# A graph attention layer on one core: layer norm in four parts, GpSimd as a helper, q through four banks, and x in groups of four at the end

## The chip, the cores and the metric

The kernel runs on one NeuronCore of a Trainium2 chip. The metric is the device time of one execution in microseconds (us); the median of several executions is compared. Engines are named as in the profile: PE (TensorE matmul), PEld (its weight loads), DVE (VectorE), ACT (ScalarE), POOL (GpSimd) and SP (SyncE, which here only starts transfers).

## What is computed

x has 6250 rows (nodes) of 256 columns. There are 200000 edges, sorted by destination. Cut to what matters:

```python
h = jnp.maximum(_layernorm(x, axis=-1), 0.0)
q = linear(h, wq, bq)
k = linear(h, wk, bk)
v = linear(h, wv, bv)
scores = jnp.sum(q[dst] * k[src], axis=-1) * scale
scores = scores + (edge_weight[:, None] @ we + be)[:, 0]
# softmax of the scores over the edges of each destination, then
out = jax.ops.segment_sum(v[src] * attn[:, None], dst, num_segments=n)
y = layer_norm(h + out + linear(h, ws, bs), g1, b1)
ffn = linear(jax.nn.gelu(linear(y, w_ff1, b_ff1)), w_ff2, b_ff2)
result = x + layer_norm(y + ffn, g2, b2)
```

## The kernel before, in words

The 6250 rows are handled as B = 49 blocks of 128 (the last has 106). The program has three parts in a row; between two of them all engines meet.

**The first part** makes h and q. SP loads x into `acc` in four transfers of 12 blocks (`x_in[0..3]`), then the edge lists: `src` and the edge weights by rows, and `dst` twice (`dst_a` on 125 partitions, `dst_b` on 124 and 1). DVE measures 24 blocks (bn_stats, L485), computes mean and deviation (`layer_variance`, the square root on ACT in `layer_deviation`, `layer_factors`, L240 to L263), and ACT normalises block after block with the ReLU fused (L419), counting `h_done`. A loop of 49 turns (one a block) follows. In a turn PE transposes h of the next block (L625) and multiplies (bias L633, weights L635) to q in PSUM bank 2 or 3; DVE copies the transpose to SBUF (`copy_hT`, L492); ACT and DVE split q into three bf16 parts in a chain of four (ACT L426, DVE L502, ACT L430, DVE L496). The first nine turns also measure three of the other 25 blocks each (L521), and ACT normalises two or three blocks a turn. At fixed turns the edge lists are turned on PE (L640) and copied, and a plan of steps is computed (from turn PLAN + 2, PLAN = 13). SP stores h to DRAM in 13 transfers of four blocks (`store_h`, L294; the last has one), in order, each as soon as its blocks are done.

POOL casts the destinations (L358), compares chunk ends (L363, L364), clears the first 12 blocks of `acc` (`clear(0)`, L380), waits until all of h is in DRAM (`h_out`), starts 32 gathers of h rows for the first eight chunks of edges (L388) and clears the rest of `acc` (L380). Then the part ends.

**The second part** goes over the edges: 391 chunks of 512, in some 440 steps. POOL starts four gathers a chunk (L788); SP tells DVE when a chunk has landed (L752) and POOL when one of eight slots is free (L756).

**The third part** goes over the 49 blocks again. In its first loop PE multiplies the sums with wv (L1393), and DVE adds a row block read back from DRAM (`r_rows`, L1273, four in flight). The second loop is the feed forward (PE L1385, L1411, L1419; ACT L1170; POOL L1231, L1235; DVE L1312, L1318 and bn_stats L1285). In its last 16 turns (MIXED) the final layer norm is applied to two blocks a turn: ACT normalises to `z_unit` (L1165), POOL adds b2 to x read again from DRAM (L1242, into `x_b2`), DVE multiplies by g2 (`scale_z`, L1330) and adds (`add_x`, L1336), SP stores (L1121). x is loaded a block at a time (L1125), and x, `x_b2`, `z_unit` and the output rows each have four slots. When the last block of the second loop has been measured, its deviation and factors follow, and then the last 17 blocks go through the same four operations.

Of the kernel before, what the change touches and what calls it, by code (L numbers as in the profile page):

```python
# [29 lines left out]
def ceil_div(a, b):  # L30
    return -(-a // b)


def gnn_layer(nc, x, src, dst, edge_weight, wq, bq, wk, bk, wv, bv, ws, bs, we, be, g1, b1, g2, b2,
# [22 lines left out]
    XH = 2 * XG  # L57
    MEASURED = ceil_div(B - XH, 3)
    PLAN = 13
# [8 lines left out]
    with ctx:  # L68
# [74 lines left out]
        q_bias = q_rest[:, 1, :]  # L143
# [21 lines left out]
        bias_rest = part(D1)  # L165
        assert used[0] <= ROWS and 3 * HEAD <= 6 * D
# [43 lines left out]
        h_done, hT_ready, hT_copied = sem("h_done"), sem("hT_ready"), sem("hT_copied")  # L210
        h_out = [sem(f"h_out{k}") for k in range(5)]
        q_ready, hi_done, rest_done, mid_done, lo_done = (sem(n) for n in ("q_ready", "hi_done", "rest_done", "mid_done", "lo_done"))
# [15 lines left out]
        def columns(v, n):  # L228
            return v.rearrange("(c p) -> p c", p=P)

# [44 lines left out]
        with nc.Block() as block:  # L275
            @block.sync
            def _(sp):
# [13 lines left out]
                def store_h(k):  # L291
                    first, end = 4 * k, min(4 * k + 4, B)
                    sp.wait_ge(h_done, end)
                    sp.dma_start(h_rows[first * P:end * P, :].rearrange("(b p) d -> p b d", p=P), acc[:, first:end, 0:D]).then_inc(h_out[k // 3], 16)  # L294
# [7 lines left out]
                for k in range(ceil_div(B, 4)):  # L302
                    store_h(k)
# [8 lines left out]
            def _(pool):  # L312
# [44 lines left out]
                pool.wait_ge(list_in, 3 * 16)  # L357
                g.tensor_copy(dst_s[0:EDGE_P, :], dst_a[0:EDGE_P, :]).then_inc(dst_cast, 1)  # L358
# [6 lines left out]
                last.then_inc(ends_compared, 1)  # L365
                pool.wait_ge(tab_copied, 2)
# [15 lines left out]
                clear(0)  # L382
# [6 lines left out]
                for k in range(1, 5):  # L389
                    clear(k)  # L390

            @block.scalar
            def _(act):
# [20 lines left out]

                def normalise(first, end):
                    for b in range(first, end):
                        if b == XH:
                            act.wait_ge(ln_done, 2)
                        nc.scalar.activation(acc[:, b, 0:D], acc[:, b, 0:D], ACT.Relu, bias=nmr[:, b:b + 1], scale=rstd[:, b:b + 1]).then_inc(h_done, 1)  # L419

                def normalised(b):
                    return min(B, 4 + 2 * b if 4 + 2 * b <= XH else XH + 3 * (b - (XH - 4) // 2))

                def first_part(b):
                    act.wait_ge(q_ready, b + 1)
                    nc.scalar.copy(q3[:, b, 0, 0:D1], banks[2 + b % 2][:, 0:D1]).then_inc(hi_done, 1)  # L426
# [9 lines left out]
                act.wait_ge(ln_done, 1)  # L436
                normalise(0, 3)
                first_part(0)
                normalise(3, 4)
                for b in range(1, B):  # L440
                    second_part(b - 1)
# [3 lines left out]
                    normalise(normalised(b - 1), normalised(b))  # L445
                    if b == 4:
                        act.wait_ge(src_in, 3 * 16)
                        nc.scalar.copy(src_f, src_i).then_inc(src_cast, 1)
                    if b == 11:
# [5 lines left out]
                    if b == 13:  # L455
# [3 lines left out]
                    if b == MEASURED:  # L459
                        layer_deviation(act, 1, XH, B)  # L460
# [3 lines left out]
            def _(dve):  # L464
# [17 lines left out]
                for k in range(2):  # L482
                    dve.wait_ge(x_in[k], 16)
                    for b in range(k * XG, (k + 1) * XG):
                        last = nc.vector.bn_stats(stats[:, b, :], acc[:, b, 0:D])  # L485
                last.then_inc(stats_done, 1)
                layer_variance(dve, 0, 0, XH)
                layer_factors(dve, 0, 0, XH)

                def copy_hT(b):  # L490
                    dve.wait_ge(hT_ready, b + 1)
# [6 lines left out]
                def what_is_left(b):  # L498
# [3 lines left out]
                    nc.vector.tensor_tensor(q_rest[:, b % 2, :], banks[2 + b % 2][:, 0:D1], q3[:, b, 0, 0:D1], ALU.subtract).then_inc(rest_done, 1)  # L502
# [8 lines left out]
                for b in range(B):  # L511
                    if b + 1 < B:
                        copy_hT(b + 1)
                    if b >= 1:
                        third_part(b - 1)
                    what_is_left(b)
                    if b < MEASURED:
                        for other in range(XH + 3 * b, min(XH + 3 * b + 3, B)):
                            if other % XG == 0:
                                dve.wait_ge(x_in[other // XG] if other < FULL else x_rest_in, 16)  # L520
                            last = nc.vector.bn_stats(stats[:, other, :], acc[:, other, 0:D])  # L521
                    if b == MEASURED - 1:
                        last.then_inc(stats_done, 1)
                        layer_variance(dve, 1, XH, B)
                    if b == MEASURED:
                        layer_factors(dve, 1, XH, B)
                    if b == 7:
# [3 lines left out]
                    if b == 9:  # L531
# [928 lines left out]
```

## Time and profile before

| | |
|---|---|
| median of 3 runs | 2411.99 us (2410.64 to 2416.51) |
| the profiled execution's own time | 2409.18 us |
| its span, first to last instruction | 2407.3 us |
| busy share | PE 92%, PEld 77%, DVE 73%, POOL 68%, ACT 48% |
| mean granted TensorE clock | 0.983 of full speed |
| first layer norm: variance, square root and factors of 24 blocks | 21.20 to 23.46 us, first normalise at 23.49 |
| end of the q loop (its last DVE operation) | 127.2 us |
| first instruction of the second part | 133.2 us |
| end of DVE's longest wait for r, at block 4 | 2121.2 us |
| normalising one of the last blocks on ACT, start to start | 0.51 us |

The busy shares are means over three parts with different limits. The rows below are read by stretch. Lines (L388) are those of the kernel before; a releaser behind "<-" is the instruction or transfer whose end ended an idle time.

### The profile page before, as it was taken

Reading aid. Unit: us, or ns where it says so; the run is one execution under the profiler, and the core shown is the slowest. Engines: PE = TensorE matmul, PEld = TensorE weight load, DVE = VectorE, ACT = ScalarE, POOL = GpSimd, SP = SyncE. Lnnn points to the kernel's source line nnn. Section 1 sums busy time; section 2 is a strip of 40 time slices with the busy share of each in tenths; the row PEclk is TensorE's granted clock in tenths of the full one; section 3 lists DMA queues with packets and bytes.
Section 4 is the critical chain, followed back from the end, with each engine's and each line's share of the span. In section 5 each row is a group of like instructions: output and inputs, shape, how many; then the busy total and the mean of one; then the engine's idle time right before and its main releaser. Section 6 shows DMA issues by size and latency. Waiting matters only on the chain. (4 is left out here: it accounts for less than half of the span.)

```text
span 2407.3 us, 70152 instructions
## 1 busy us (share of the span) xinstructions
PE 2209.0 (92%) x14709; PEld 1864.0 (77%) x14710; DVE 1753.2 (73%) x7374; ACT 1166.4 (48%) x2875; POOL 1631.0 (68%) x1817
## 2 busy tenths in 40 slices
PE   5779989899999999999999999999999999989994
PEld 4568777777777777877888888888888888877883
DVE  6768667676777777777777877787778887784367
ACT  5545444444444444444444544555545555554454
POOL 3457777777777777777777777777777777402355
PEclk8989999999999999999999999999999999999997
DMA  7434444444444444444444444444444444340024
GB/s 228 135 95 137 137 137 138 139 137 136 137 137 139 136 137 136 139 137 137 139 137 138 138 139 137 138 137 139 137 139 137 139 137 139 93 138 5 0 62 143
DMA packets 148690, 311.05 MB, mean 129 GB/s; under 512 B 34127, under 2 KB 85186, under 8 KB 148665
## 3 DMA queue, kind: packets, MB, share of 16 engines
q0 software_dynamic: 75264, 205.62, 29.1%
q1 hardware_dynamic: 55278, 90.19, 11.4%
q10 hardware_dynamic: 18122, 14.96, 2.0%
q8 instruction: 9, 0.15, 0.0%
q14 instruction: 17, 0.13, 0.0%
HBM read 290.21 MB, written 20.43 MB: 129 GB/s over the span
## 5 line engine op out<-in xcount | busy, mean ns | idle before, releaser
L788 POOL DMA_INDIRECT work<-h_rows,idx x1536 | 1458.5, 950 | 483.0 <-issue 446.4
L876 PE MATMUL bank<-work 128*128 x3520 | 836.4, 380 | 0.0
L967 DVE SCALAR_TENSOR_TENSOR work<-bank,work 128x257 bf16<-128x257 f32 x1764 | 646.8, 425 | 232.9 <-SPq L752 201.6
L813 PE MATMUL bank<-q,onehot 128*128 x5304 | 739.4, 274 | 62.1 <-DVE work L967 50.1
L876 PEld LDWEIGHTS bank<-work 128*128 128x128 f32 x3520 | 634.8, 190 | 78.6
L813 PEld LDWEIGHTS bank<-q,onehot 128*128 128x128 bf16 x5304 | 509.2, 98 | 146.9 <-issue 84.8
L924 ACT COPY work<-bank 128x256 f32<-128x256 f32 x880 | 285.4, 377 | 397.8 <-PE bank L863 393.8
L920 ACT ACTIVATE work<-work 128x1 f32<-128x1 f32 x440 | 129.6, 295 | 622.9 <-DVE work L1033 622.9
L1033 DVE CUSTOM_DVE_ANT_0 work<-bank,work 128x512 f32<-128x512 f32 x440 | 329.8, 750 | 106.1 <-PE bank L819 75.8
L921 ACT ACTIVATE work<-work 128x512 f32<-128x512 f32 x440 | 311.6, 708 | 0.0
L863 PE MATMUL bank<-ident,work 128*128 128x128 f32 x1760 | 266.7, 274 | 29.5 <-ACT work L921 29.5
L819 PE MATMUL bank<-ident,work 128*128 128x128 f32 x1764 | 273.1, 277 | 16.7 <-DVE work L973 7.8
L890 ACT ACTIVATE work<-onehot 128x512 bf16<-128x512 bf16 x442 | 284.6, 644 | 1.6 <-DVE onehot L956 1.6
L863 PEld LDWEIGHTS bank<-ident,work 128*128 128x128 f32 x1760 | 212.7, 140 | 86.0 <-ACT work L921 51.5
L819 PEld LDWEIGHTS bank<-ident,work 128*128 128x128 f32 x1764 | 195.2, 136 | 67.4 <-issue 39.7
L956 DVE TENSOR_SCALAR onehot<-dst_words,node 128x512 bf16 x443 | 167.8, 379 | 74.2 <-issue 48.5
L984 DVE SCALAR_TENSOR_TENSOR acc<-acc,work,bank 128x257 f32 x441 | 211.9, 480 | 8.8 <-issue 3.2
L967 DVE DVE_READ_ACCUMULATOR work<-bank,work 128x1 f32 x1764 | 145.2, 82 | 0.0
L973 DVE TENSOR_TENSOR work<-work,ew_all 128x4 f32<-128x4 f32 x441 | 73.6, 167 | 80.3 <-DVE work L967 38.2
L1170 ACT ACTIVATE work<-bank,bff_col 128x128 f32<-128x128 f32 x196 | 55.9, 369 | 98.6 <-PE bank L1411 98.6
L1411 PE MATMUL bank<-work,dst_words 128*128 128x128 f32 x784 | 97.4, 278 | 2.7 <-DVE work L1312 2.6
L1235 POOL TENSOR_TENSOR work<-work 128x256 f32<-128x256 f32 x49 | 35.7, 729 | 90.2 <-DVE acc L1318 88.2
(190 smaller groups left out, 1570.0 us busy)
## 6 DMA issues: line engine op xcount, KB each, us to landing
dst_words<-dst_short SPq DMA_DIRECT2D x99, 512.0 KB
work<-h_rows,idx POOLq DMA_INDIRECT x1568
bias<-h_rows ACTq DMA_DIRECT2D x56, 128.0 KB
r_rows<-bias ACTq DMA_DIRECT2D x55, 128.0 KB
work<-r_rows SPq DMA_DIRECT2D x49, 128.0 KB, 2.0
acc<-in_x SPq DMA_DIRECT2D x4, 1536.0 KB, 15.4
h_rows<-acc SPq DMA_DIRECT2D x12, 512.0 KB, 4.6
work<-in_x SPq DMA_DIRECT2D x48, 128.0 KB, 2.1
```

The source lines that it names most:

```text
L788: pool.indirect_dma_start(rows[:, u, j, 0:D], None, h_rows, bass.IndirectOffsetOnAxis(idx[:, half, u * J + j:u * J + j + 1], 0)).then_inc( ...
L813: last = nc.tensor.matmul(banks[j][:, 0:D1], onehot[:, k, j, :], q3[:, bass.ds(b, 1), c, 0:D1], start=(c == 0), stop=(c == 2))
L819: last = nc.tensor.transpose(banks[4][:, j * P:(j + 1) * P], score[:, k, j:j + 1].broadcast_to([P, P]), ident[:])
L863: last = nc.tensor.transpose(banks[5 - half][:, j * P:(j + 1) * P], probsT[:, (2 * half + j) * P:(2 * half + j + 1) * P], ident[:])
L876: last = nc.tensor.matmul(banks[6 + k][:, 0:D1], probs[:, j, :], rows[:, bass.ds(slot, 1), j, :], start=(j == 2), stop=(j == 1))
L890: nc.scalar.activation(outside[:, k, :], onehot[:, k].rearrange("p j n -> p (j n)"), ACT.Copy, scale=BIG, bias=-BIG).then_inc(outside_done, 1)
L921: nc.scalar.activation(probsT, masked, ACT.Exp, bias=new_max, scale=-1.0).then_inc(exp_done, 1)
L924: nc.scalar.copy(probs[:, 2 * half:2 * half + 2, :].rearrange("p j n -> p (j n)"), banks[5 - half][:, 0:2 * P]).then_inc(probs_done, 1)
L956: nc.vector.tensor_scalar(onehot[:, k], dst_of[:, bass.ds(at, C)].rearrange("p (j n) -> p j n", j=J), node[:, bass.ds(b, 1)], None, ALU.is ...
L967: last = nc.vector.scalar_tensor_tensor(out=product[:, j, 0:D1], in0=banks[j][:, 0:D1], scalar=SCALE, in1=rows[:, bass.ds(slot, 1), j, :], ...
L984: nc.vector.scalar_tensor_tensor(out=a, in0=a, scalar=decay[:, k:k + 1], in1=banks[6 + k][:, 0:D1], op0=ALU.mult, op1=ALU.add).then_inc(ad ...
L1033: nc.vector.tensor_tensor_reduce(out=masked, in0=banks[4][:], in1=outside[:, k, :], scale=-1.0, scalar=old_max[:, k:k + 1], op0=ALU.add, o ...
```

## The change

In the first part the layer norm is done in four parts (12, 12, 12 and 13 blocks) in place of two. The first needs only the first transfer of x. DVE measures four blocks a turn. POOL normalises blocks 40 to 47, in two groups of four: four times scale and shift, then one maximum with zero over the four; ACT normalises the other 41, three a turn. The cast of `src` goes from ACT to POOL. POOL compares the chunk ends ahead of its waits for the lists, and `clear(0)` goes behind the gathers. q goes through banks 2 to 5, and every step of the split comes a turn or two later in its engine's order. From block 14 on, ACT copies the transposes in place of DVE. The plan starts three turns later (PLAN = 16).

In the third part the r blocks have eight slots in place of four, so do `z_unit` and the output rows (which share the r slots). x comes in groups of four blocks, three groups in flight; b2 is added in place, and a group's slot is loaded again once the last of its four blocks has been added. `layer_variance` of the last 17 blocks goes ahead of the last turn's `scale_z` and `add_x`. The loops of the last stage are written out.

```diff
-    XH = 2 * XG
-    MEASURED = ceil_div(B - XH, 3)
-    PLAN = 13
+    QUARTERS = [(0, XG), (XG, 2 * XG), (2 * XG, 3 * XG), (3 * XG, B)]
+    BY_POOL = range(FULL - 8, FULL)
+    BY_ACT = 14
+    PLAN = 16
+        VARIANCE_AT = [ceil_div(end - XG - 10, 4) for first, end in QUARTERS[1:]]
+        DEVIATION_AT = VARIANCE_AT
@@ SP: the stores of h @@
-                for k in range(ceil_div(B, 4)):
-                    store_h(k)
+                for first in range(0, BY_POOL[0], 4):
+                    store_h(first, first + 4)
+                for first in (BY_POOL[0], BY_POOL[0] + 4):
+                    store_h(first, first + 4)
+                    if first == BY_POOL[0]:
+                        store_h(B - 1, B)
@@ POOL @@
-                pool.wait_ge(list_in, 3 * 16)
-                g.tensor_copy(dst_s[0:EDGE_P, :], dst_a[0:EDGE_P, :]).then_inc(dst_cast, 1)
                 pool.wait_ge(plan_consts, 1)
...
                 last.then_inc(ends_compared, 1)
+                pool.wait_ge(src_in, 3 * 16)
+                g.tensor_copy(src_f, src_i).then_inc(src_cast, 1)
+                pool.wait_ge(list_in, 3 * 16)
+                g.tensor_copy(dst_s[0:EDGE_P, :], dst_a[0:EDGE_P, :]).then_inc(dst_cast, 1)
+
+                pool.wait_ge(ln_done, 4)
+                for n, half in enumerate((BY_POOL[0:4], BY_POOL[4:8])):
+                    for b in half:
+                        last = g.tensor_scalar(acc[:, b, 0:D], acc[:, b, 0:D], rstd[:, b:b + 1], nmr[:, b:b + 1], ALU.mult, ALU.add)
+                    last.then_inc(scaled, 1)
+                    pool.wait_ge(scaled, n + 1)
+                    g.tensor_scalar(acc[:, half[0]:half[-1] + 1, 0:D], acc[:, half[0]:half[-1] + 1, 0:D], 0.0, None, ALU.max).then_inc(h_done_by_pool, 4)
...
-                clear(0)
                 for k in range(4):
                     pool.wait_ge(h_out[k], 3 * 16)
...
-                for k in range(1, 5):
+                for k in range(5):
                     clear(k)
@@ ACT @@
+                def copy_hT(b):
+                    act.wait_ge(q_ready, b - 1)
+                    act.wait_ge(hT_ready, b + 1)
+                    nc.scalar.copy(hT[:, b % 2, :], banks[b % 2][:, 0:D]).then_inc(hT_copied_by_act, 1)
...
-                layer_deviation(act, 0, 0, XH)
+                layer_deviation(act, 0, *QUARTERS[0])
                 normalise(0, 3)
-                first_part(0)
-                normalise(3, 4)
-                for b in range(1, B):
-                    second_part(b - 1)
+                for b in range(B):
+                    if BY_ACT <= b + 1 < B:
+                        copy_hT(b + 1)
+                    if b >= 2:
+                        second_part(b - 2)
...
                     first_part(b)
-                    normalise(normalised(b - 1), normalised(b))
+                    if b in DEVIATION_AT:
+                        turn = DEVIATION_AT.index(b) + 1
+                        layer_deviation(act, turn, *QUARTERS[turn])
+                    normalise(3 * b + 3, 3 * b + 6)
@@ DVE @@
+                measure(0, XG)
+                layer_variance(dve, 0, *QUARTERS[0])
+                measure(XG, XG + 2)
+                layer_factors(dve, 0, *QUARTERS[0])
+                measure(XG + 2, XG + 6)
...
-                    if b + 1 < B:
+                    if b + 1 < BY_ACT:
                         copy_hT(b + 1)
+                    if b >= 3:
+                        third_part(b - 3)
                     if b >= 1:
-                        third_part(b - 1)
-                    what_is_left(b)
+                        what_is_left(b - 1)
+                    measure(XG + 6 + 4 * b, XG + 10 + 4 * b)
@@ PE @@
                 def project(b):
-                    k = b % 2
-                    pe.wait_ge(hT_copied, b + 1)
-                    if b >= 2:
-                        pe.wait_ge(rest_done, b - 1)
+                    q = banks[2 + b % 4][:, 0:D1]
+                    copied(b)
+                    if b >= 4:
+                        pe.wait_ge(rest_done, b - 3)
...
                 for b in range(B):
-                    if b + 1 < B:
-                        transpose_h(b + 1)
+                    if b + 2 < B:
+                        transpose_h(b + 2)
                     project(b)
@@ third part @@
+        RING = 8
+        X_GROUPS = 3
-        r_in = slots(4, D)
+        r_in = slots(RING, D)
-        x_again = slots(4, D)
-        x_b2 = r_in
-        z_unit = slots(4, D)
+        x_again = slots(4 * X_GROUPS, D)
+        z_unit = slots(RING, D)
-        o_rows = slots(4, D)
+        o_rows = r_in
@@ SP @@
+                for b in range(B):
+                    n = rows_of(b)
                     sp.wait_ge(o_done, b + 1)
+                    sp.dma_start(out[b * P:b * P + n, :], o_rows[0:n, b % RING, :]).then_inc(o_stored[b % RING], 16)
+                    if b % 4 == 3 and b // 4 + X_GROUPS <= B // 4:
+                        load_x(b // 4 + X_GROUPS)
@@ POOL @@
-                def add_b2(b, at):
-                    n = rows_of(at)
-                    if not (isinstance(b, int) and b < 4):
-                        pool.wait_ge(o_done, b - 3)
-                    pool.wait_ge(x_back[at % 4], turn4(b, at) * 16 + 32)
+                def add_b2(b):
+                    n, k, g = rows_of(b), b % (4 * X_GROUPS), b // 4
+                    pool.wait_ge(x_back[g % X_GROUPS], 16 + g // X_GROUPS * 16 + 16)
+                    nc.gpsimd.tensor_tensor(x_again[0:n, k, :], x_again[0:n, k, :], row_of["b2"][0:n], ALU.add).then_inc(x_b2_done, 1)
@@ DVE, in the last turns @@
                     if b == B - 1:
                         last.then_inc(stats_done, 1)
+                        layer_variance(dve, 7, EARLY, B)
```

## Rows read from the trace of the kernel before

**Rows 1.** Stretches of the span: busy us (instructions) per engine, granted clock, DMA share, GB/s.
```profile
152.30:2082.00 1929.70, 1836.92 (x12499) 1555.34 (x12497) 1444.60 (x6491) 930.35 (x2272) 1468.68 (x1584) 1.00 0.45 138
...
2381.00:2403.00 22.00, 0.00 (x0) 0.00 (x0) 15.52 (x34) 9.08 (x17) 8.97 (x13) 0.50 0.52 160
```

**Rows 2.** Timeline of POOL in the first part: start, us, instruction, count, wait before.
```profile
48.64 1.52 POOL L358 CAST q<-q 125x1600 int16<-125x1600 int32 x1 [28.43 <-DMA q<-in_dst]
...
81.14 1.18 POOL L388 DMA_INDIRECT work<-h_rows,idx  x1 [21.88 <-DMA h_rows<-acc]
...
121.84 8.37 POOL L380 MEMSET acc<- 128x3084 f32 x4
...
152.35 0.95 POOL L788 DMA_INDIRECT work<-h_rows,idx  x1 [22.15 <-SPq L756]
```

**Rows 3.** Groups on POOL from 48 to 131: busy, mean ns | idle before.
```profile
L388 POOL DMA_INDIRECT work<-h_rows,idx x32 | 31.3, 977 | 31.3 <-DMA h_rows<-acc 21.9 <-issue 8.8 <-PE bank L625 0.6
L380 POOL MEMSET acc<- 128x3084 f32 (+1 forms) x5 | 11.0, 2258 | 0.0
L363 POOL TENSOR_SCALAR onehot<-dst_words,work 128x128 bf16<-128x128 f32 x4 | 2.7, 666 | 0.1
```

**Rows 4.** Waits from 200 to 2050: us in total, times, longest.
```profile
DVE work L967 <- SPq L752: 199.5, 167, 2.5
```

**Rows 5.** Timeline of ACT and SP: the last normalise, and the stores of h.
```profile
75.44 0.60 ACT L419 ACTIVATE acc<-acc,nmr,rstd 128x256 f32<-128x256 f32 x1
...
50.34 26.08 SPq L294 DMA_DIRECT2D h_rows<-acc  x8
```

**Rows 6.** Stretches after the lists have landed, columns as in Rows 1.
```profile
48.60:52.00 3.40, 1.16 (x6) 0.85 (x5) 3.33 (x8) 1.57 (x4) 3.27 (x5) 0.86 0.84 290
52.00:57.00 5.00, 4.25 (x20) 3.42 (x18) 1.62 (x5) 2.32 (x6) 4.91 (x11) 0.75 0.30 104
57.00:60.00 3.00, 1.43 (x11) 1.37 (x12) 1.16 (x3) 3.00 (x8) 2.25 (x1) 1.00 0.00 0
```

**Rows 7.** Timeline of DVE in the first part.
```profile
12.32 4.01 DVE L485 BATCH_NORM_STATS2 stats<-acc 128x6 f32<-128x256 f32 x12 [4.11 <-DMA acc<-in_x]
...
31.46 0.42 DVE L496 TENSOR_TENSOR q<-work,q 128x257 bf16<-128x257 f32 x1
...
32.13 1.07 DVE L521 BATCH_NORM_STATS2 stats<-acc 128x6 f32<-128x256 f32 x3
...
33.44 0.42 DVE L496 TENSOR_TENSOR q<-work,q 128x257 bf16<-128x257 f32 x1
...
48.84 1.35 DVE L261 SCALAR_TENSOR_TENSOR nmr<-mean,rstd 128x25 f32<-128x25 f32 x1
```

**Rows 8.** Timeline of PE in two turns late in the q loop.
```profile
120.55 1.03 PE L635 MATMUL bank<-work 128*128 128x257 f32 x4
...
121.80 1.03 PE L635 MATMUL bank<-work 128*128 128x257 f32 x4
```

**Rows 9.** Waits from 2109 to 2126, the start of the third part.
```profile
DVE work L1273 <- DMA work<-r_rows: 6.4, 4, 3.8
```

**Rows 10.** Timeline of DVE from the last feed forward turn to the end.
```profile
2376.26 0.74 DVE L1330 TENSOR_TENSOR work<-work,bias 128x256 f32<-128x256 f32 x2
...
2377.59 0.18 DVE L240 TENSOR_TENSOR mean<-stats 128x17 f32<-128x17 f32 x1
...
2381.22 0.85 DVE L1330 TENSOR_TENSOR work<-work,bias 128x256 f32<-128x256 f32 x2 [1.15 <-ACT work L1165]
...
2401.99 0.75 DVE L1336 TENSOR_TENSOR work<-work 128x256 f32<-128x256 f32 x2
```

**Rows 11.** Groups from 2381 to 2403: busy, mean ns | idle before, releasers.
```profile
L1330 DVE TENSOR_TENSOR work<-work,bias 128x256 f32<-128x256 f32 (+1 forms) x17 | 10.1, 592 | 7.1 <-DMA out<-work 4.2 <-ACT work L1165 2.8
...
L1242 POOL TENSOR_TENSOR work<-work,bias 128x256 f32<-128x256 f32 (+1 forms) x13 | 9.0, 690 | 12.0 <-DMA work<-in_x 8.8 <-DVE work L1336 3.2
L1336 DVE TENSOR_TENSOR work<-work 128x256 f32<-128x256 f32 (+1 forms) x17 | 7.0, 414 | 0.0
```

More of the change, by code:

```diff
@@ L511, in _ @@
                 for b in range(B):
-                    if b + 1 < B:
+                    if b + 1 < BY_ACT:
                         copy_hT(b + 1)
+                    if b >= 3:
+                        third_part(b - 3)
                     if b >= 1:
-                        third_part(b - 1)
-                    what_is_left(b)
[L517 to L527, printed above, removed]
+                        what_is_left(b - 1)
+                    measure(XG + 6 + 4 * b, XG + 10 + 4 * b)
+                    if b in VARIANCE_AT:
+                        turn = VARIANCE_AT.index(b) + 1
+                        layer_variance(dve, turn, *QUARTERS[turn])
+                    if b - 1 in VARIANCE_AT:
+                        turn = VARIANCE_AT.index(b - 1) + 1
+                        layer_factors(dve, turn, *QUARTERS[turn])
+                    if b == 11:
                         dve.wait_ge(tab_turned, 1)
@@ L1196, in mixed @@
-                def mixed(i, j):
-                    b, at = i * 2 + (B - MIXED + j), B - MIXED + j
-                    if not (isinstance(i, int) and b + 1 >= B):
-                        gelu(b + 1, at + 1)
-                    if not (isinstance(i, int) and b + 3 >= B):
+                layer_deviation(act, 6, 0, EARLY)
+                for j in range(MIXED):
+                    b = B - MIXED + j
+                    if b + 1 < B:
+                        gelu(b + 1, b + 1)
+                    if b + 3 < B:
@@ L1209, in _ @@
[L1209 to L1220 removed]
+                        last_unit(2 * j + c, 2 * j + c)
@@ L1222, in _ @@
+                layer_deviation(act, 7, EARLY, B)
+                act.wait_ge(ln_done, 8)
+                for b in range(EARLY, B):
+                    last_unit(b, b)
             @block.gpsimd
@@ L1348, in mixed @@
-                def mixed(i, j):
-                    b, at = i * 2 + (B - MIXED + j), B - MIXED + j
-                    if not (isinstance(i, int) and b + 2 >= B):
-                        copy_yT(b + 2, at + 2)
-                    last = second_sum(b, at)
-                    if isinstance(i, int) and b == B - 1:
+                layer_factors(dve, 6, 0, EARLY)
+                for j in range(MIXED):
+                    b = B - MIXED + j
+                    if b + 2 < B:
+                        copy_yT(b + 2, b + 2)
+                    last = second_sum(b, b)
+                    if b == B - 1:
@@ L1365, in _ @@
-                if MIXED > 2:
-                    for j in range(2):
-                        mixed(MIXED // 2 - 1, j)
-                layer_variance(dve, 5, EARLY, B)
-                layer_factors(dve, 5, EARLY, B)
-                scale_z(EARLY, EARLY)
-                def third_sum(b, at):
-                    scale_z(b + 1, at + 1)
-                    add_x(b, at)
-                over(dve, EARLY, B - 2, 4, third_sum)
-                third_sum(B - 2, B - 2)
-                add_x(B - 1, B - 1)
+                            step(2 * j + c)
@@ L1380, in _ @@
+                layer_factors(dve, 7, EARLY, B)
+                scale_z(EARLY)
+                for b in range(EARLY, B - 1):
+                    scale_z(b + 1)
+                    add_x(b)
+                add_x(B - 1)
             @block.tensor
```

217 lines of the change are left out of this document (100 added, 117 removed).

## The prediction

> **What bounds the kernel now.** I read the stretches of the span first, then POOL's timeline, then who waits for what at the start and at the end.
>
> From 152.3 to 2082 us the edges are worked through [rows 1]. PE is busy 95% of it, but a busy PE in this profile is not one at its peak; POOL is busy 1468.7 of 1929.7 us with 0.3 us of issue between two gathers, and DVE waits 199.5 us for chunks that have not landed [rows 4]. 1536 gathers in 1929 us are 1.257 us each, the bare pitch of a gather (0.95 and 0.30). So POOL's gathers set the pace there. The change touches nothing in this part: it moves as a block, and only when it may begin counts, and how long the rest takes behind it.
>
> When it begins is POOL's timeline [rows 2]: POOL gets the destination lists at 48.64 (28.4 us of waiting), then waits again until 81.14 for the last h in DRAM, starts 32 gathers until 121.84, and clears until 130.21. The engines meet, the second part opens near 133, and POOL's next gather is at 152.35, when the first steps have freed a slot. The q loop on the other engines ends about 127, 3 us ahead of POOL. The reader is to see two things: between last h and first gather lie 5.1 us (76.04 to 81.14: store, landing, wake up) [rows 2, 5], and the last h is late because ACT normalises the last block at 75.44 [rows 5].
>
> At the end, the last 17 blocks take from 2381.2 to 2402.74, 1.27 us a block, with no engine full: DVE 15.5 of 22 us, ACT 9.1, POOL 9.0 [rows 1]. The waits go round in a ring of four slots: POOL for x, DVE for stored output, ACT for DVE [rows 11].
>
> **The change, first part.** The start of the loop: 12 blocks are measured by 16.33 [rows 7]; variance, square root and factors took 2.3 us before for 24, so ACT can normalise from about 19 in place of 23.5. A turn of DVE is three operations at 0.33 and three measurements at 0.36, pitch 1.98 (31.46 to 33.44) [rows 7]; with four measurements it is 2.35, and eight such turns with three rounds of variance and factors (about 2 us each) end near 46. Then `ln_done` is 4, ahead of POOL, which has the lists at 48.64 and cast by 50.15. ACT's turns with three blocks are 2.1 to 2.2 us; its last block of 41 comes in turn 12, about 55.
>
> POOL then has eight scale operations of 256 columns. No row shows one. The nearest is the compare, 0.67 us for 128 columns with one column scalar [rows 3]: bounds 0.67 and 1.33; I take 0.85, since the cast runs 1600 columns in 1.52 us [rows 2], so that the columns cost less than what is fixed. The two maxima over 1024 columns: 0.97 each at the rate of the cast, 5.3 at that of the compare; I take 1.5. Sum 8 x 0.85 + 2 x 1.5 = 9.8 (7.3 to 21.4), done at 60.0 (57.5 to 71.6). With the 5.1 us of the last store this allows gathers at 65.1.
>
> The stores have a bound of their own. Six of them, 24 blocks, were issued by 50.34 [rows 5], and moved until 57.0: between 52 and 57 the DMA share is 0.30 at 104 GB/s, then zero [rows 6]. A few of the 16 DMA engines worked on, which the lists had held until 48.64. 24 blocks in 8.4 us on the fullest are 0.35 us a block; now nearly all 49 are issued by then, which makes 17.1 us: 65.7, and some 0.9 us to the wake up, 66.7. I take 66.7 for the first gather (66 to 76.7).
>
> The Trainium skill (DMA: Bandwidth & Descriptors, Why a DMA increments its semaphore by 16 and not by 1) says that a transfer uses the largest number of engines up to 16 that divides its slowest dimension: 125 partitions give 5, 124 give 4. The share of 0.30 agrees. Without such a queue on few engines the first gather would come at 65.1 in place of 66.7, and the sum would be 1.6 us lower.
>
> The moved clear costs 2.68 us behind the gathers (8.37 us for the four others; 11.0 for all) [rows 2, 3]. It was hidden before in the wait for h. POOL's end: 66.7 + 40.7 + 11.05 = 118.4 against 130.21: **11.8 us earlier** (1.8 to 12.5).
>
> What else must be ready by then: PE's pitch late in the loop is 1.25 us a turn (120.55 to 121.80), and PE is back to back there [rows 8]. From turn 13, near 58, 35 turns at 1.25 are 43.8, and 7 for the edge lists, the plan and its waits: 109, 9 us ahead of POOL. With four banks PE has three turns of slack over DVE's plan, ACT's copies are 0.85 us a turn; I cost these edits at nothing because POOL covers them. Without the cover the loop would set the end (rival 1). The `src` cast on POOL (1.6 us) lies in its wait for the lists, the idle 28.4 us; so do the eight compares, 5.1 us that stood behind the lists before. Behind POOL's normalising wait the index copies and the addition to ws (1.3 us); they must precede the gathers but fit before 66.7. SP sends the short destinations after the last h store, 14 us sooner than before.
>
> DVE and POOL disturb each other: DVE's L261, two inputs in SBUF, on 25 columns took 1.35 us over POOL's cast at 48.84 [rows 2, 7]. In turns 8 to 13 DVE has 1 us of work in 2.2 us, so I cost it at nothing.
>
> **The change, third part.** At its start DVE waited up to 3.8 us for r block 4 [rows 9], behind weights, biases and 0.5 MB of x. Now eight r blocks come first, but 1.5 MB of x stands before the ninth: 4.1 MB in place of 2.7 from 2109. At the rate of before (2.7 MB in 12 us) it lands about 2127, and is wanted about 2121. The stall moves and stays; I take 0 (2 gained to 2 lost, the clock included).
>
> The end: the four operations in the last turn took 1.33 us (2376.26 to 2377.59), 0.333 each [rows 10]. `layer_variance` ahead of them hides the 0.4 us for which DVE waited for the square root: first `scale_z` at 2380.8 in place of 2381.22. Then with eight slots nobody waits in a ring. DVE has 34 operations at 0.333: 11.3 us. ACT (0.51 a block) is faster. POOL has added b2 up to block 39 by then; blocks 40 to 43 are loaded after store 31 (about 2379), 44 to 47 after store 35 (about 2384.5), some 4.5 us before DVE wants them. Nine additions on POOL fall in this stretch. What one costs DVE: L1330 had 592 ns where 407 to 414 is the clear value [rows 11], 17 x 0.18 = 3.1 us over 13 additions, 0.24 each: 2.2 us; if DVE is full, up to one more operation each, 0.45: 4.1. I take 3.1. Last `add_x` at 2380.8 + 11.3 + 3.1 = 2395.2, not 2402.74: **7.5 us** (4.5 to 10.6). The tail of 4.6 us behind it stays. In the 16 mixed turns PE sets the pace and keeps it: 0 (1 gained, 2 lost, as DVE is nearly full there).
>
> The Trainium skill (SBUF — State Buffer, SBUF: two separate sides) says that a VectorE operation with two SBUF inputs and a GpSimd operation that reads SBUF exclude each other for the whole instruction. By it nine additions would cost 9 x 0.64 = 5.8 us in place of 3.1, and the sum would be 2.7 us higher. The rows show less.
>
> **Sum.** 11.8 + 7.5 = 19.3 us. Of the span 2407.3 that leaves 2388.0, of the profiled execution's own 2409.18 it leaves 2389.9; the median was 2.8 higher: 2392.7, so **2393 us**.
>
> **Rivals.** (1) The q loop ends the first part. From turn 21 to 49 it ran at 1.85 us a turn (75.4 to 127.2, stalls of the plan in it); if slack doesn't help, 35 turns from 58 end at 122.7: gain 7.5 in place of 11.8, 2397. For it: DVE's plan holds it 6 us at one place; against: a bare turn is 1.25. Chance 0.14. (2) POOL is slow at elementwise work: the upper prices, 21.4 us, gathers at 76.7, gain 1.8: 2403. 0.10. (3) The end runs without disturbance, and x and stores flow: 3 us more: 2390 or 2389. 0.15. (4) The other side: POOL's ten operations stand on the path that ends the first part. They decide once they take 50.15 to 80.8, 31 us, over three times my price, since then 2.68 of the clear and a first gather at 85.9 eat the 7.5 of the end. At 3.5 us a block it is slower by some 2 us, and with a spoilt end by more: 2414 to 2420. Nothing in the rows is so slow. 0.06. (5) The gains are there but small, both at their lower bounds and with a longer stall for r: under 7.2 us, 2406. 0.07. The rest, 0.48, is the forecast: 2388 to 2399.
>
> 0.3% is 7.2 us, about what a measurement of this kernel can tell from no change. Faster by more: the forecast and rivals 1 to 3, 0.87, less some doubt for what I have not seen: 0.85. Same 0.09, slower 0.06. The range 2385 to 2403 holds the forecast, rivals 1 and 3, and just rival 2.
>
> **What would show it.** First L388-like gather at 65 to 69, last clear ending 117 to 120, the second part's first gather near 140.5; last `add_x` 14 to 16 us after the first `scale_z` of the last 17; the wait for r at the start of the third part still 3 to 5 us, now once for block 8. I am wrong if POOL's scale takes over 1.5 us, if a POOL wait for lists or h grows, if ACT or PE stalls in the first turns on the new order, or if the second part does not keep its 1929 us.

## The result and the profile after

The changed kernel takes 2404.01 us (median of 5 runs, 2402.30 to 2404.72); the kernel before takes 2412.68 us beside it (2410.64 to 2416.51). The ratio is 0.9958, 95% interval 0.9947 to 0.9969: faster by 8.7 us in the medians (10.1 by the ratio), where 19 were forecast. 2404.01 us lies 1.0 us above the upper end of the forecast range, 2403. The profiled execution took 2402.3 us with a span of 2400.5, 6.8 us under the span of before.

POOL's timeline in the first part after the change (start, us, instruction, wait before):

```profile
48.97 1.52 POOL L378 CAST q<-q 125x1600 int16<-125x1600 int32 x1 [15.91 <-DMA q<-in_dst]
50.48 2.56 POOL L383 TENSOR_SCALAR acc<-acc,rstd,nmr 128x256 f32<-128x256 f32 x4
53.20 2.77 POOL L386 TENSOR_SCALAR acc<-acc 128x1024 f32<-128x1024 f32 x1 [0.16 <-POOL acc L383]
55.96 2.47 POOL L383 TENSOR_SCALAR acc<-acc,rstd,nmr 128x256 f32<-128x256 f32 x4
58.59 2.88 POOL L386 TENSOR_SCALAR acc<-acc 128x1024 f32<-128x1024 f32 x1 [0.16 <-POOL acc L383]
...
66.52 1.75 POOL L408 DMA_INDIRECT work<-h_rows,idx  x1 [3.57 <-issue]
...
108.27 10.97 POOL L401 MEMSET acc<- 128x3084 f32 x5
141.44 0.95 POOL L831 DMA_INDIRECT work<-h_rows,idx  x1 [22.19 <-SPq L799]
```

Against [rows 2] the first gather comes at 66.52 in place of 81.14, POOL ends at 119.24 in place of 130.21, and the second part's first gather is 10.9 us sooner. The ten operations of POOL take 50.48 to 61.47, 11.0 us: the four scales 0.63 apart, the maximum 2.8. The q loop's last DVE operation ends at 110.8, 8.5 us ahead of POOL.

The first part came out as forecast. So the loss is behind it. Both traces laid side by side at the same points of the program give a ledger (us; plus is gained):

| stretch | forecast | before to after | measured |
|---|---|---|---|
| up to the second part's first gather | +11.8 | 152.35 to 141.44 | +10.9 |
| from there to its last gather | 0 | 1929.4 to 1932.4 long | -3.0 |
| to the third part's first transfer | 0 | 27.2 to 26.4 | +0.8 |
| first loop of the third part, up to PE's 0.68 us wait for DVE late in it | 0 | 59.3 to 62.6 | -3.4 |
| up to the turn in which PE waits for ACT's first `z_unit` | 0 | 149.0 to 147.6 | +1.4 |
| mixed turns, to the last first-layer matmuls (2369.07, now 2367.38) | 0 | 51.9 to 56.9 | -5.0 |
| to the first `scale_z` of the last 17 | +0.4 | 12.2 to 12.8 | -0.7 |
| to the end of the last `add_x` | +7.1 | 21.5 to 15.8 | +5.7 |
| sum | +19.3 | | +6.8 |

Two stretches of the third part that were costed at nothing took 8.4 us. The first is the start of the third part; the waits of DVE from 2100 to 2122 (us in total, times, longest), and DVE's timeline there:

```profile
DVE work L1305 <- DMA work<-r_rows: 8.1, 4, 5.3
```

```profile
2119.02 0.48 DVE L1305 SCALAR_TENSOR_TENSOR work<-bias,work 128x256 f32<-128x256 f32 x1 [5.34 <-DMA work<-r_rows]
```

In [rows 9] the longest was 3.8. It now comes once, for block 8, as forecast, but 18.9 us after the first transfer; block 4 came 12.3 us after it before, and four blocks at 1.09 us behind that make 16.7. That is 2.1 of the 3.4 us. Behind the wait PE worked at a granted clock of 0.50 (the lower of its two levels, 1.2 GHz) for some 6.8 us, where it was 3.4 before; a block took PE up to 2.13 us there in place of 1.09, and this makes some 1.2 more. The stretches, columns as in [rows 1], after and before:

```profile
2119.00:2125.70 6.70, 5.73 (x16) 4.54 (x17) 4.98 (x13) 1.56 (x4) 0.00 (x0) 0.50 0.39 120
```

```profile
2123.00:2126.20 3.20, 3.20 (x11) 2.54 (x10) 2.33 (x8) 0.85 (x3) 0.00 (x0) 0.50 0.39 121
...
2177.70:2180.90 3.20, 3.00 (x15) 2.70 (x13) 0.48 (x4) 0.56 (x2) 0.00 (x0) 0.50 0.03 5
```

The 1.4 us gained in the next stretch is the clock as well. Before, PE's first 16 matmuls of the second loop ran at 0.50 (2177.7 to 2180.9) and took 3.46 us; after, they ran at 1.00 and took 2.02, behind the same wait of 2.6 us. No edit aimed at this. Both timelines of PE, before and after:

```profile
2177.24 3.46 PE L1411 MATMUL bank<-work,dst_words 128*128 128x128 f32 x16 [2.59 <-DVE work L1312]
```

```profile
2171.89 2.02 PE L1429 MATMUL bank<-work,dst_words 128*128 128x128 f32 x16 [2.60 <-DVE work L1344]
```

The second stretch is the mixed turns. DVE, POOL and PE after the change, one turn each (three timelines):

```profile
2344.62 0.72 DVE L1344 TENSOR_SCALAR work<-bank,g_col,b_col 128x128 f32<-128x128 f32 x2
2345.26 0.41 DVE L1350 TENSOR_TENSOR acc<-bank,work 128x256 f32<-128x256 f32 x1
2345.71 0.43 DVE L1317 BATCH_NORM_STATS2 stats<-acc 128x6 f32<-128x256 f32 x1
2346.05 1.49 DVE L1362 TENSOR_TENSOR work<-work,bias 128x256 f32<-128x256 f32 x2
2347.46 1.63 DVE L1368 TENSOR_TENSOR work<-work 128x256 f32<-128x256 f32 x2
2349.02 0.72 DVE L1344 TENSOR_SCALAR work<-bank,g_col,b_col 128x128 f32<-128x128 f32 x2
```

```profile
2345.75 0.73 POOL L1275 TENSOR_TENSOR work<-work 128x256 f32<-128x256 f32 x1 [1.33 <-DVE acc L1350]
2346.43 1.60 POOL L1280 TENSOR_TENSOR work<-work,bias 128x256 f32<-128x256 f32 x2
2347.99 0.82 POOL L1271 TENSOR_TENSOR work<-work,bias 128x256 f32<-128x256 f32 x1
```

```profile
2345.40 2.05 PE L1429 MATMUL bank<-work,dst_words 128*128 128x128 f32 x16 [0.18 <-DVE work L1344]
```

DVE has no idle time left: 0.64 + 0.45 + 0.34 + 1.41 + 1.56 = 4.40 us, and PE waits for it in 12 turns (2.6 us in all; its weight loads wait 5.8 us in 13). Its last four operations (L1362, L1368) would be 0.334 apart; they are 0.63 to 0.78 apart, and POOL's four operations stand beside them without a gap. Before, the same turn (from 2342.26) had both `scale_z` 0.33 apart, since POOL was waiting 1 us for x then, and only both `add_x` were slow.

At the end (DVE's timeline) the ring is gone, as forecast, and the disturbance is there for a stretch:

```profile
2386.06 0.42 DVE L1362 TENSOR_TENSOR work<-work,bias 128x256 f32<-128x256 f32 x1
2387.00 0.84 DVE L1368 TENSOR_TENSOR work<-work 128x256 f32<-128x256 f32 x1 [0.53 <-POOL work L1280]
2387.77 0.85 DVE L1362 TENSOR_TENSOR work<-work,bias 128x256 f32<-128x256 f32 x1
...
2393.22 0.41 DVE L1368 TENSOR_TENSOR work<-work 128x256 f32<-128x256 f32 x1
```

Eight operations stand 0.78 apart in place of 0.334: 3.6 us, with eight of POOL's nine additions beside them. The forecast had 3.1.

The first of the nine shows the disturbance from the other side:

```profile
2383.45 3.52 POOL L1280 TENSOR_TENSOR work<-work,bias 128x256 f32<-128x256 f32 x1 [5.21 <-DMA work<-in_x]
```

It took 3.52 us in place of 0.63 (the shortest of these additions). DVE's operations beside it, from 2383.37 to 2386.06, stayed 0.334 apart; DVE stopped at 2386.5 to wait for its result, and the addition ended at 2387.0. So it is not always DVE that pays: here a close row of DVE operations held POOL up.

### The profile page after: what moved, and what is told of

The parts are those of the page before. It is cut to its first block and busy times, and to the rows that moved or that the text cites. A ratio compares the mean times of both kernels' runs of the same rounds, so it can differ in the third digit from the quotient of the medians.

```text
span 2400.5 us, 69609 instructions
## 1 busy us (share of the span) xinstructions
PE 2212.3 (92%) x14709; PEld 1867.1 (78%) x14710; DVE 1757.4 (73%) x7359; ACT 1168.5 (49%) x2903; POOL 1653.7 (69%) x1828
## 5 line engine op out<-in xcount | busy, mean ns | idle before, releaser
L1010 DVE SCALAR_TENSOR_TENSOR work<-bank,work 128x257 bf16<-128x257 f32 x1764 | 646.7, 424 | 231.7 <-SPq L795 200.3
L1010 DVE DVE_READ_ACCUMULATOR work<-bank,work 128x1 f32 x1764 | 144.8, 82 | 0.0
```

The costliest lines, as they stand in the source:

```text
L1010: last = nc.vector.scalar_tensor_tensor(out=product[:, j, 0:D1], in0=banks[j][:, 0:D1], scalar=SCALE, in1=rows[:, bass.ds(slot, 1), j, :], ...
```

## The experiments

All kernels of this section bound the registers that are loaded from memory and then waited on, and this slows the second part in three different ways (below). So each is compared with the control of its own group, and the stretches of the first and third part are read from the traces; the bounding stands in none of their loops. The granted clock can still differ there from kernel to kernel.

**Controls.** e0: each loaded value masked where it is used. e4: masked once. e8: the three tables held as 16 bits, no mask, so that no instruction is added.

```diff
@@ e0 @@
-                return eng.snap(eng.to_reg(step >> (BLOCKS.bit_length() - 1)), min_val=0, max_val=B * TP + U)
+                return eng.snap(eng.to_reg((step >> (BLOCKS.bit_length() - 1)) & 32767), min_val=0, max_val=B * TP + U)
@@ e4 @@
+                        dve.reg_alu(regs[u], loaded[u], 32767, ALU.bitwise_and)
@@ e8 @@
-        steps_tab = sb("steps_tab", [1, HEAD], I32)
+        steps_tab = sb("steps_tab", [1, HEAD], mybir.dt.uint16)
```

> The changed kernel with one addition that all experiments have: each register that is loaded from memory and later waited on is masked with a constant first, one or two register operations more per load on SP, DVE, ACT, PE and POOL. Theory A (POOL's gathers set the pace of the second part, so register work on the other engines is hidden): within 1 us of the changed kernel, 2403 to 2406. Rival (a register operation on DVE or SP lies on the path of a step): 440 steps times 0.05 us, up to 22 us more.

> The changed kernel again, with the masks made light: each loaded register is masked once, by one register operation, where it is first wanted (DVE 10 more instructions in the loop of eight steps in place of 32, SP 8 in place of 20). Theory A (the size of DVE's loop or the masks right after the load made the first control slow, 3 us a turn of the loop): below 2440. Rival B (each register operation on DVE costs its time): 10 operations in place of 32 leave a third of the 167 us, near 2460. First and third part as in the changed kernel: first gather near 67, last clear near 119.5, third part 300 to 301 us.

> The changed kernel with its three tables of steps held as unsigned 16 bits, which are loaded without any mask: not one instruction more than in the changed kernel. Theory A (the two earlier controls were slow because DVE's loop of eight steps grew from 289 to 299 and 321 instructions, with a gap of 3 to 5 us at each turn of the loop): the gap is gone and the time is that of the changed kernel, 2402 to 2406. Rival (the masks' register operations themselves, wherever they stood): the same outcome, so this run does not part the two; if it is still slow, it was neither.

Measured: e0 2571.80 us (2569.45 to 2574.37), e4 2597.24 (2591.11 to 2601.68), e8 2463.76 (2462.97 to 2464.30). All three expectations missed in size. Third part 300.6, 303.1 and 300.3 us, 300.3 in the changed kernel (why e4's is longer is shown at e5); last clear at 120.1, 120.2 and 120.3. The waits of DVE at the head of its loop over 1000 us of the second part, in e0, e4 and e8, with a second wait that is long in e0 alone:

```profile
DVE work L1076 <- issue: 89.7, 26, 4.9
DVE work L1010 <- issue: 57.3, 178, 0.6
```

```profile
DVE work L1087 <- issue: 93.7, 25, 5.4
```

```profile
DVE work L1016 <- issue: 61.0, 27, 2.5
...
DVE work L1076 <- issue: 11.0, 27, 0.4
```

DVE's loop of eight steps has 321 instructions in e0 and 299 in e4 by my count, and DVE stands 3.5 and 3.7 us (mean) at each turn of it; with 289 (e8, and the changed kernel) it stands 0.4. e0 also waits 0.3 us at 178 places in these 1000 us (L1010). The masks in e0 and e4 also read registers that have just been loaded, and e8 has no masks. So whether the number of instructions or the masks make DVE stand is not shown; nor is it why e4, with fewer masks, is 25 us slower than e0. e8 has a stall of its own, 2.3 us a turn, behind the load of twelve 16-bit values.

**One part of the change alone.** e1 and e10: the new first part with the old third part. e2: the old first part with the new third part.

> The new first part with the old third part. Ledger theory (the two traces laid side by side: the second part's first gather came 10.9 us sooner, all of the third part's edits together cost 1.9 us in the span): 2400 to 2403, as good as or better than the whole change, the second part opening near 122.4 and the mixed turns at the old pitch of 3.945 us. Rival (the sooner start is partly given back by the second part itself, which took 2.2 to 3.0 us longer from its first gather on): then the gain is 8 to 9 us, 2403 to 2405, with the same 2 to 3 us in the second part's length as in the whole change. If the second part has its old length here, its lengthening was no effect of the first part.

> The old first part with the new third part. Ledger theory: the third part costs 1.9 us more than it saves, so 2412 to 2416 against 2412.7 of the kernel before: no gain at all from the longer rings. In its trace: mixed turns at 4.395 us, the longest wait for r about 5.3 us, the last 17 blocks in about 15.7 us. Prediction's theory: 7.5 us faster, 2405. Rival on the clock: the losses in the third part hang on when it starts; then the pitch of the mixed turns is 3.945 here.

> The new first part with the old third part, 16-bit tables. Old third part: 298.4 us in the trace of before, 304.7 in the first run of this combination. Theory A (its length hangs on when x lands beside DVE's operations, so it varies from kernel to kernel): third part between 298 and 305, mixed turns between 3.95 and 4.3 us, time 2400 to 2408. Rival (its length is 298.4 and the 304.7 came of the slow loop of the second part): 298 to 299, time 2400 to 2402.

Measured: e1 2574.39 us (2565.92 to 2581.24) beside e0's 2571.80; e10 2461.62 (2460.73 to 2467.76) beside e8's 2463.76; e2 2584.69 (2581.69 to 2589.03) beside 2571.80. So the new first part is worth 12.9 us in the medians (e2 against e0; in their traces POOL's first gather of the second part comes 9.2 us sooner, 153.19 to 143.98, and e2's second part is 3.4 us longer), and the new third part between +2.6 and -2.1, nothing that can be told. e2 also has the 4.395 us turns, a longest wait for r of 5.28 and 15.8 us for the last 17, though it starts its third part at another time: the losses belong to the third part's own edits. The old third part took 298.4, 304.7 and 299.8 us in before, e1 and e10. Its mixed turns differ too (3.945 was expected for e1), 3.97, 4.12 and 4.07 us in the mean over 13. POOL's timeline in e1, two turns:

```profile
2510.69 0.82 POOL L1285 TENSOR_TENSOR work<-work,bias 128x256 f32<-128x256 f32 x1 [1.71 <-DMA work<-in_x]
...
2514.02 0.89 POOL L1285 TENSOR_TENSOR work<-work,bias 128x256 f32<-128x256 f32 x1 [0.27 <-DMA work<-in_x]
```

POOL waits 1.7 us for x in one turn and 0.3 in the next, and with the short wait one of DVE's two `scale_z` is slow too (0.78 us to the next operation in place of 0.334). The old kernel's pitch thus hung on when a transfer landed.

**The wait for r.** e3: x behind the r blocks.

```diff
-                for g in range(X_GROUPS):
-                    load_x(g)
                 def next_r(b, at):
...
                 over(sp, 0, B - RING, RING, next_r)
+                for g in range(X_GROUPS):
+                    load_x(g)
```

> The three first groups of x (1.5 MB) are loaded behind all r blocks in place of ahead of the ninth. Theory A (these 1.5 MB are what r block 8 waits for): the 5.3 us wait goes down to under 1.5 us and the time falls by 3.5 to 5 us against the control. Rival B (the weights, 1 MB for the feed forward and 0.25 MB for wv, and the eight r blocks themselves fill the queue): the wait falls by less than 2 us. Rival C (PE at the lower clock at the start of the third part sets the pace): the wait goes, but PE's matmuls take its place and less than 1.5 us is gained.

Measured: 2567.93 us (2567.51 to 2570.30) beside 2571.80. The third part is 294.1 us in place of 300.6. The waits of DVE at its start:

```profile
DVE acc L1311 <- PE bank L1411: 2.6, 3, 1.4
DVE work L1305 <- DMA work<-r_rows: 2.5, 3, 1.2
```

The wait of 5.0 us for block 8 is gone and 6.4 us with it. The other 1.4 us is the clock: e0's was 0.50 behind the wait, from 2289.2 to 2292.4, and e3's is 1.00 there. In e0 and in e3:

```profile
2289.20:2292.40 3.20, 3.05 (x8) 2.48 (x9) 2.56 (x8) 0.52 (x2) 0.00 (x0) 0.50 0.40 112
```

```profile
2285.00:2295.00 10.00, 10.00 (x56) 8.55 (x56) 9.96 (x29) 7.28 (x19) 0.00 (x0) 1.00 0.47 135
```

Theory A holds: it was the 1.5 MB of x ahead of block 8. Rivals B and C allowed at most 2 us. In the medians 3.9 us are left of the 6.4; the second part was 4.0 us longer in e3's trace (2083.3 and 2079.3 us from first to last gather).

**The mixed turns.** e5: POOL's additions held until DVE is at its operations on PSUM. e6: no additions.

```diff
-                    scale_y(B - MIXED + j, B - MIXED + j)
+                    nc.gpsimd.tensor_tensor(y_g1[:, k, :], unit[:, k, :], row_of["g1"], ALU.mult).then_inc(g1_done, 1)
+                    if j >= 3:
+                        pool.wait_ge(o_done, 2 * (j - 2))
                     for c in range(2):
                         add_b2(2 * j + c)
+                    pool.wait_ge(z_done, b - 1)
+                    nc.gpsimd.tensor_tensor(y_rows[:, k, :], y_g1[:, k, :], b1_bff2, ALU.add).then_inc(y_ready, 1)
```

> POOL's two b2 additions of a mixed turn stand ahead of the y addition and wait until DVE has ended add_x of the turn three before, so that they run beside DVE's operations with an input in PSUM (1.1 us a turn) in place of its scale_z and add_x. Theory A (a POOL addition and a DVE operation with two SBUF inputs slow each other, and that alone stretches the turn): the mixed turns fall from 4.395 us to PE's 3.945 to 4.0, the third part gets 5 to 7 us shorter, 293.5 to 295.5. Rival B (the loops written out, or the stores in a row on SP, stretch the turn): the pitch stays at 4.395. Rival C (the held additions come too late for y or add_x): pitch over 4.4 and a wait of DVE on POOL.

> Left out: POOL adds no b2 to x at all, DVE adds the bare x. It shows what the additions cost DVE in all. Theory A (contention): scale_z and add_x in the mixed turns at 0.33 to 0.45 us each with only POOL's two y operations beside them, pitch 3.945; the last 17 blocks with all 34 operations at 0.334 us, 11.4 us or a little more in place of 15.7; third part 290 to 292 us. Rival B: pitch 4.395 still. Rival C (x arrives late at the end: POOL waited 5.2 us for a group): the last 17 blocks stay over 13 us with a wait of DVE for x.

Measured: e5 2589.55 us (2587.93 to 2590.91) beside e4's 2597.24; third part 293.9 in place of 303.1. Of these 9.2 us the held additions gave 6.4: from the first `scale_z` to the end e5 takes 83.2 us and e4 89.6 (e0 too). The other 2.7 us come ahead of the mixed turns, and are the clock: at the start of the second loop PE was granted 0.50 for some 10 us in e4 and 3.4 in e5. In e4 and in e5:

```profile
2366.30:2376.30 10.00, 8.28 (x34) 7.60 (x34) 0.90 (x3) 3.29 (x11) 0.63 (x1) 0.50 0.01 2
```

```profile
2364.40:2367.60 3.20, 2.85 (x14) 2.55 (x12) 0.44 (x3) 0.66 (x3) 0.00 (x0) 0.50 0.02 5
2367.80:2374.40 6.60, 5.43 (x39) 4.89 (x40) 1.92 (x6) 2.74 (x9) 1.47 (x3) 1.00 0.00 0
```

e6 has one run, 2588.92; third part 290.5. Both e5 and e6 have turns of 3.945 us. DVE and POOL in a turn of e5:

```profile
2532.19 1.49 DVE L1383 TENSOR_TENSOR work<-work,bias 128x256 f32<-128x256 f32 x2
2533.60 0.75 DVE L1389 TENSOR_TENSOR work<-work 128x256 f32<-128x256 f32 x2
2534.27 0.72 DVE L1365 TENSOR_SCALAR work<-bank,g_col,b_col 128x128 f32<-128x128 f32 x2
2535.33 0.42 DVE L1371 TENSOR_TENSOR acc<-bank,work 128x256 f32<-128x256 f32 x1 [0.34 <-PE bank L1458]
```

```profile
2531.89 0.73 POOL L1310 TENSOR_TENSOR work<-work 128x256 f32<-128x256 f32 x1 [0.17 <-DVE acc L1371]
2532.58 0.81 POOL L1303 TENSOR_TENSOR work<-work,bias 128x256 f32<-128x256 f32 x1
2534.43 1.23 POOL L1293 TENSOR_TENSOR work<-work,bias 128x256 f32<-128x256 f32 x2 [1.03 <-DVE work L1389]
```

The additions now run beside L1365, which reads PSUM: they take 0.62 us each in place of 0.80, L1365 keeps its 0.72, and both L1389 are 0.34 apart. DVE waits 0.34 us for PE again. Only where the additions stand was changed, so theory A holds and the written-out loops (rival B) are cleared. In e6 the last 17 blocks take 14.0 us in place of 15.8, with every DVE operation 0.334 apart and 2.2 us of waits for stores (0.35 and 1.86 us), where theory A expected 11.4 us and rival C a wait for x: the additions cost 1.8 us there net, because without them the stores become the limit.

**Together.** e7 and e9: x late, additions held, and `clear(0)` back ahead of the gathers, in two groups. e11: e9 with ACT normalising all 49 blocks.

```diff
+                clear(0)
                 for k in range(4):
                     pool.wait_ge(h_out[k], 3 * 16)
...
-                for k in range(5):
+                for k in range(1, 5):
                     clear(k)
```

> Three edits at once, each to be read in its own place: x loaded behind the r blocks, the additions held, and the clear of the first twelve blocks back ahead of the gathers. Sum of the theories: third part 6.4 us shorter from x (as in the earlier run), 5 to 7 from the held additions, 300.5 to 287 to 290; last clear at about 117 in place of 119.7, since POOL waits 4.7 us for the last h there and the clear takes 2.7. Against the light control 14 to 16 us less. Rival: the stalls hide each other, less than 10 us; or the clear ahead of the gathers pushes the first gather back by up to 2.7 us and gives nothing.

> The three edits of the earlier combined run (x behind the r blocks, additions held, first clear ahead of the gathers), with the 16-bit tables. From the stretches measured before: third part 288.0 against 300.3 to 300.5, last clear 116.6 against 119.7, so 12.4 + 3.1 = 15.5 us below the control: 2387 to 2391. Rival (the sooner end of POOL's first part is given back in the second part, where DVE, PE and POOL are all close to full): 12.4 alone, 2391 to 2394.

> The mended kernel with ACT normalising all 49 blocks; POOL's ten elementwise operations (10.9 us) are gone. Theory A (POOL's help takes the last h from ACT's path): ACT's turns of three blocks go on until turn 15, each now with a copy of a transpose too, last h near 63 to 64, first gather at 68.5 to 70 in place of 67, time 1 to 3 us over the mended kernel. Rival B (POOL's ten operations, done at 61.4, set the first gather no sooner than ACT could): first gather within 1 us of 67, no difference in the time. Rival C (POOL slows DVE and ACT in the first turns): faster by 1 us or more.

Measured: e7 2577.59 us (2573.97 to 2583.19), 19.7 below e4, where 14 to 16 were expected. Its third part is 288.0, 15.1 us shorter, and 2.7 of these are e4's lower clock; its second part is 4.8 us shorter (2100.4 and 2105.2), which nothing here explains. e9 2447.03 (2446.50 to 2448.75), 16.7 below e8, with a second part of the same length (1971.8 and 1971.7 us between the first and the last gather). e9's third part is 287.5 in place of 300.3: 6.4 us up to the first `scale_z` and 6.4 behind it. Its last clear ends at 116.67 in place of 120.27. POOL in e9:

```profile
61.36 2.67 POOL L401 MEMSET acc<- 128x3084 f32 x1
65.48 2.82 POOL L409 DMA_INDIRECT work<-h_rows,idx  x1 [1.46 <-issue]
```

The clear fits into the wait for the last h. e11: 2448.59 us (2448.39 to 2451.61), 1.6 more than e9; the last normalise ends at 62.7 on ACT, the first gather starts at 69.66 and the last clear ends at 119.26, 2.6 us later. So POOL's eight blocks are worth about 2 us; the rest of the first part's gain comes from the quarters, the order of the turns and the banks, which no run here parts.

No kernel ran with these edits and the second part as in the changed kernel. Taken off its 2404 us, the 16.7 us of e9 would give an estimate of 2387.

## Why the prediction was right in direction and half as large

- **First part (11.8): right.** 10.9 us in the traces of before and after, 9.2 in those of e2 and e0. POOL's ten operations took 11.0 us, not 9.8: the scales less than my 0.85 (0.63), the maxima nearly twice my 1.5 (2.8). The first gather at 66.5 was forecast at 66.7. POOL's own end plus 5.1 us gives 66.6, so the trace does not tell whether the stores' few DMA engines or POOL set it.
- **The cover of the q loop: right.** It ended at 110.8, forecast 109, so rival 1 fell. POOL was not slow (rivals 2 and 4).
- **The moved clear: right in price, needless.** "The moved clear costs 2.68 us": e9's clear costs nothing where it stood before.
- **Second part (0): open.** 3.0 us longer in the profile. "If the second part does not keep its 1929 us" was one of my signs of being wrong, and it came. Among kernels with the same second part the length between first and last gather differs without regard to the first part: 2079.3, 2084.2, 2082.7 (this one with the old first part) and 2083.3 us in e0 to e3. Nothing shows that the change did it.
- **Third part's start (0, "2 gained to 2 lost"): the step that failed.** "It lands about 2127, and is wanted about 2121" was nearly right: 18 us after the first transfer, and 18.9 were measured. But those two numbers are a wait of 6 us against 3.8 before, and I took 0. 3.4 us were lost, 2.1 by the later block and 1.2 by the lower clock behind it; e3 shows that x ahead of block 8 made the wait, and that 6.4 us were to be had there. The 1.4 us gained at the start of the second loop are luck: the clock stayed at 1.00, which no edit aimed at. Against the 1.2 us lost behind the wait the clock comes out about even.
- **The mixed turns: the other step that failed**, and the larger one. "In the 16 mixed turns PE sets the pace and keeps it: 0 (1 gained, 2 lost, as DVE is nearly full there)." I looked for what DVE's work was, not for what POOL did beside it once x never made it wait. Before, POOL's 1 us of waiting kept one addition off DVE's `scale_z`. With x always there, all four operations stand 0.63 to 0.78 us apart and DVE's turn grows from under 3.95 to 4.40: 5.0 us. e5 and e6 show it. I had used the same effect at the end (3.1 us) and not here.
- **The end (7.5): 5.0.** The last 17 took 15.8 us, within the 14 to 16 forecast and 1.4 over the sum: eight disturbed operations 3.6 us, where 3.1 stood, 0.6 us at the wait for POOL's 3.52 us addition, and 0.2 us of the first pair. The moved variance lost 0.7 where 0.4 was to be gained: POOL's additions ran beside it too.
- **Rivals 2 and 5** (2403 and 2406) have the times nearest to the result, and neither for its reason. POOL's operations took 11.0 us, not rival 2's 21.4; and no gain was at its lower bound, as rival 5 has it: two costs that I had put at nothing stood against them. My range reached to 2403 for rival 2's sake, so that the result lies so near to it is luck. 2388 to 2399, the forecast's own span, was missed by 5 us.

The disturbance itself: the Trainium skill (SBUF — State Buffer, SBUF: two separate sides) says that a VectorE operation with two SBUF inputs and a GpSimd operation that reads SBUF exclude each other for the whole instruction. The rows agree in kind: the operations of the two engines alternate, and the addition that met a close row of DVE operations took 3.52 us. By the rule a pair would take some 0.334 + 0.63 = 0.96 us, an estimate from the durations of these rows; the pairs here took 0.78.

## What to carry to other kernels

A wait that is taken away from a helper engine lets its work slide somewhere: look at what will stand beside it before you cost the edit at nothing, above all where the two engines disturb each other. Such work can be held, on purpose, beside the other engine's PSUM operations; in e5 it cost DVE nothing there. Transfers that are wanted late go behind those that are wanted soon, even when all of them are "prefetch".

## What the runs showed of the hardware

- DVE stands 0.4 us at the head of its loop of the second part with 289 instructions (e8 and the changed kernel), and in the mean 3.7 us (up to 5.4) with 299 (e4) and 3.5 with 321 (e0). Not shown: whether the number of instructions does it or the masks on freshly loaded registers, which only the two slow loops have.
- Twelve table entries of 16 bits, loaded into DVE's registers once a loop, hold DVE for 2.3 us (e8); twelve of 32 bits show no such wait (the changed kernel).
- A POOL addition of 256 columns takes 0.62 us beside a DVE operation that reads PSUM and 0.80 beside one that reads SBUF twice; the DVE operations then stand 0.78 us apart in place of 0.334. An addition that came between DVE operations 0.334 apart took 3.52 us, and left them as they were.
- POOL's maximum over 1024 columns took 2.8 us (0.69 for each 256) and its scale and shift of 256 columns 0.63. These are different operations; a maximum over 256 columns was not run.
- The granted clock in the third part was not the same from kernel to kernel where the code was: at the start of the second loop it was 0.50 for about 3.4 us (before, e0, e5), about 10 us (e4), or not at all (after). Between e4 and e5 this made 2.7 us.
